# Two graph layers on one core: the first row of every adjacency loaded and split once, with a new order of all queues

## What is computed

```python
# x [128,128,512], adj [128,128,128]
# layer 0
h = maximum(layernorm(x), 0)
A_hat = adj + eye; d = A_hat.sum(-1) ** -0.5
x = x + (A_hat * d[:, :, None] * d[:, None, :]) @ (h @ W + b)

# layer 1
h = maximum(layernorm(x), 0)
H = (adj != 0); w = adj[:, 0, :]                 # row 0 of each adjacency: one weight per edge
Dn = where(H @ w > 0, 1 / (H @ w), 0); Be = 1 / H.sum(axis=1)
conv(x, W, b) = Dn * (H @ (Be * (H.T @ (x @ W.T)))) + b
h = relu(conv(h, W1, b1))                        # 512 -> 1024
h = layer_norm(h, gamma, beta)
out = conv(h, W2, b2) + x                        # 1024 -> 512
```

## Time and profile before

| | |
|---|---|
| median of 3 runs | 1931.68 us |
| the profiled execution | 1935.55 us |
| its span, first to last instruction | 1933.8 us |
| TensorE busy | 1874.0 us, 97% |
| DVE | 1634.2 us, 85% |
| ACT | 1445.4 us, 75% |
| POOL | 1189.7 us, 62% |
| DMA queues, share of 16 engines' span | 47.1% |
| mean granted clock of TensorE | 0.994 of full |

### The profile page before, as it was taken

The page is one execution under the profiler, slowest core; times in us unless marked ns, Lnnn a source line. Parts: engine busy times, 40 slices in busy tenths (PEclk is TensorE's granted clock), DMA queues, the critical chain, the costliest instruction groups (busy, mean ns, idle before and its releaser), DMA issues. The chain is left out here.

```text
span 1933.8 us, 37250 instructions
## 1 busy us (share of the span) xinstructions
PE 1874.0 (97%) x9926; PEld 895.9 (46%) x9926; DVE 1634.2 (85%) x3239; ACT 1445.4 (75%) x2726; POOL 1189.7 (62%) x1554
## 2 busy tenths in 40 slices
PE   5799999999999999999999999999999999999998
PEld 2344444444444444444444444444444444444443
DVE  6898888888888888888888888898888889788663
ACT  4787777777777778778778778778778778777663
POOL 4676666665665666666666666666666666566550
PEclk9899999999999999999999999999999999999999
DMA  7245554454454445544444454444454444454333
GB/s 220 46 84 109 110 107 99 102 107 99 103 112 97 102 111 101 101 109 102 102 106 101 102 109 99 102 113 96 101 111 99 101 106 109 89 108 98 70 66 77
DMA packets 536736, 197.59 MB, mean 102 GB/s; under 512 B 484944, under 2 KB 501328, under 8 KB 536528
## 3 DMA queue, kind: packets, MB, share of 16 engines
q1 hardware_dynamic: 536528, 195.21, 47.1%
HBM read 48.31 MB, written 33.55 MB: 42 GB/s over the span
## 5 line engine op out<-in xcount | busy, mean ns | idle before, releaser
L386 PE MATMUL ps_u<-w2h,raw_t 128*128 128x512 f16 x2048 | 483.9, 379 | 3.6 <-DVE raw_w L1060 3.0
L386 PEld LDWEIGHTS ps_u<-w2h,raw_t 128*128 128x128 f16 x2048 | 197.7, 98 | 232.3 <-issue 3.9
L715 ACT ACTIVATE raw_w<-raw_w 128x1024 f32<-128x1024 f32 x128 | 135.0, 1055 | 193.9 <-DVE raw_w L1011 193.1
L1423 POOL TENSOR_TENSOR base<-b_all,xh 128x512 f32<-128x512 f32 x128 | 187.1, 1462 | 90.9 <-DVE raw_w L1069 89.7
L386 PE MATMUL ps_u<-w2l,raw_t 128*128 128x512 f16 x1024 | 241.9, 379 | 0.0
L1417 POOL TENSOR_TENSOR b_all<-x,b_all 128x512 f32<-128x512 f32 x128 | 189.0, 1477 | 23.9 <-DVE x L974 13.8
L1438 POOL TENSOR_TENSOR tS<-tS 128x256 f32<-128x256 f32 x64 | 57.4, 897 | 214.4 <-ACT tS L695 214.4
L974 DVE SCALAR_TENSOR_TENSOR x<-ps_e,cx,x_t 128x512 f32<-128x512 f32 x128 | 95.0, 742 | 102.3 <-PE ps_e L439 102.2
L1055 DVE TENSOR_TENSOR bet_wide<-raw_w,bet_wide 128x1024 f16<-128x1024 f32 x128 | 157.4, 1230 | 15.1 <-ACT bet_wide L740 9.8
L1428 POOL TENSOR_TENSOR base<-base,raw_w 128x512 f32<-128x512 f32 x128 | 164.6, 1286 | 6.8 <-ACT raw_w L652 6.5
L731 ACT ACTIVATE raw_w<-raw_w,nm,sc 128x1024 f32<-128x1024 f32 x128 | 156.3, 1229 | 4.9 <-POOL nm L1499 4.9
(11 more groups left out here) (153 smaller groups left out, 4791.8 us busy)
## 6 DMA issues: line engine op xcount, KB each, us to landing
x_t<-in_x_dram SPq DMA_DIRECT2D x128, 256.0 KB, 3.0
out_dram<-raw_w SPq DMA_DIRECT2D x128, 256.0 KB, 2.3
adj_t<-in_adj_dram SPq DMA_DIRECT2D x64, 128.0 KB, 2.4
raw_t<-bet_wide SPq DMA_TRANSPOSE x256, 3.1
w_col<-in_adj_dram SPq DMA_DIRECT2D x128, 0.5 KB, 2.4
h0T_hi<-h_hi SPq DMA_TRANSPOSE x128, 2.4
h0T_lo<-h_lo SPq DMA_TRANSPOSE x128, 2.4
raw_w<-in_W1T_dram SPq DMA_DIRECT2D x4, 512.0 KB, 5.2
```

The source lines that it names most:

```text
L386: mm = pe.matmul(ps, t[:, j * 128:(j + 1) * 128], w[:, j, :], start=(n == 0 and j == 0), stop=(n == 2 and j == blocks - 1))
L715: act.activation(zh[:, g % 4, :], zh[:, g % 4, :], ACT.Relu, accum_out=hsum[:, p % 2, j:j + 1]).then_inc(s_h, 1)
L1423: pool.tensor_tensor(base[:, g % 6, :], x1b[:, :], xh[:, g % 2, :], ALU.add).then_inc(s_scr2, 1)
```

## The change

Row 0 of all 128 adjacencies is loaded in one transfer, graphs on the partitions, into the sixth slot of `base`. DVE splits it in two operations (hi and lo side by side in the same slot), and one transpose puts both halves of all graphs into a new tile WT, graph by graph in its columns. For each pair one copy, do_w(p), takes the four columns (hi and lo of two graphs) to column N of HB, a tile that now holds what HB_hi and HB_lo were. do_P(p) waits for that copy; the sixth slot of `base` is written for graph 5 by do_scr2 behind a wait for the transpose.

```diff
-    STEADY_FROM, STEADY_TO = 4, NP - 14
+    STEADY_FROM, STEADY_TO = 14, NP - 14
...
-        w_col = sb("w_col", [128, 3, 2])
+        WT = sb("WT", [128, 2, NG], F16)
...
-        HB_hi, HB_lo = sb("HB_hi", [128, 2, 2, N + 2], F16), sb("HB_lo", [128, 2, 2, N + 2], F16)
+        HB = sb("HB", [128, 2, 2, 2, N + 2], F16)
...
+        HB_hi, HB_lo = HB[:, 0, :, :, :], HB[:, 1, :, :, :]
+        w_rows = base[:, 5, 0:N]
+        w_halves = base[:, 5, N:2 * N].bitcast(F16).rearrange("p (h c) -> p h c", h=2)
...
+            def load_edge_weights():
+
+                sp.dma_start(w_rows, adj[:, 0, :]).then_inc(s_w, 16)
+
+            def turn_edge_weights():
+                sp.wait_ge(s_wrh, 1)
+                sp.wait_ge(s_wrl, 1)
+                sp.dma_start_transpose(WT[:, :, :], w_halves.rearrange("p h c -> p (h c)")).then_inc(s_wt, 16)
...
-            def do_ldw(p):
-                done(sp, s_wrl, p - 2)
-                for j in (0, 1):
-                    sp.dma_start(w_col[:, p % 3, j:j + 1], adj[2 * p + j:2 * p + j + 1, 0, :].rearrange("g e -> e g"))\
-                      .then_inc(s_w[p % 3], 16)
...
-            do_ldw(0); do_ldA(0); do_ldw(1); do_ldA(1); do_ldw(2); do_ldA(2); do_ldw(3); do_ldX(0); do_ldX(1)
-            do_ldA(3); do_trA(0)
+            do_ldA(0); do_ldA(1)
             load_weight(0, raw_w0, W, range(0, 4))
+            do_ldA(2); do_ldX(0); do_ldX(1)
             load_row(b_all, b, s_b)
             load_gamma_beta()
-            do_ldw(4); do_ldX(2); do_ldX(3); do_ldA(4); do_trA(1); do_tr0h(0); do_tr0h(1); do_tr0l(0); do_tr0l(1)
+            do_trA(0); do_ldA(3)
+            load_edge_weights()
+            do_trA(1); do_ldX(2); do_ldX(3); do_ldA(4)
             load_weight(1, raw_w1, W1T, range(0, 2))
             load_weight(1, raw_w1, W1T, range(2, 4))
-            do_ldw(5); do_ldA(5); do_trA(2)
+            do_ldA(5)
+            turn_edge_weights()
+            do_trA(2); do_tr0h(0); do_tr0h(1); do_tr0l(0); do_tr0l(1)
...
+            def split_edge_weights():
+                dve.wait_ge(s_w, 16)
+                dve.tensor_scalar(w_halves[:, 0, :], w_rows, WR_SCALE, None, ALU.mult).then_inc(s_wrh, 1)
+                dve.wait_ge(s_wrh, 1)
+                dve.scalar_tensor_tensor(out=w_halves[:, 1, :], in0=w_rows, scalar=WR_SCALE, in1=w_halves[:, 0, :],
+                                         op0=ALU.mult, op1=ALU.subtract).then_inc(s_wrl, 1)
...
-            def do_w_hi(p):
...
-            def do_w_lo(p):
...
+            def do_w(p):
+
+                if p == 0:
+                    dve.wait_ge(s_wt, 16)
+                done(dve, s_p, p - 1)
+                dve.tensor_copy(HB[:, :, p % 2, :, N], WT[:, :, 2 * p:2 * p + 2]).then_inc(s_wr, 1)
```

The tables of all five queues are new. The loop now covers k = 14 to 49, and ten of its former iterations are written out, with other orders. Its row on TensorE (M1, P, T1, ...) and its row on POOL read, in part:

```diff
-                do_M1(k); do_Y0(2 * k + 4); do_U(2 * k - 3); do_Y2(2 * k - 4); do_M5(k); do_M6(k); do_Y2(2 * k - 3)
...
+                do_M1(k); do_P(k+2); do_T1(2 * k + 2); do_Z0(2 * k + 7); do_M6(k); do_M5(k); do_M2(k)
+                do_Y0(2 * k + 8); do_Y2(2 * k - 3); do_M7(k); do_M3(k); do_T1(2 * k + 3); do_M4(k); do_Z0(2 * k + 8)
+                do_U(2 * k - 2); do_Y0(2 * k + 9); do_U(2 * k - 1); do_Y2(2 * k - 2)
```

More of the change, by code:

```diff
@@ L165, in bass_adjacency_prenorm_two_layer_gnn_kernel @@
         s_adj = [sem(f"adj_loaded_{m}") for m in range(3)]
-        s_w = [sem(f"edge_weights_loaded_{m}") for m in range(3)]
+        s_w, s_wt = sem("edge_weights_loaded"), sem("edge_weights_transposed")
         s_tra = [sem(f"A_and_H_transposed_{m}") for m in (0, 1)]
@@ L1190, in _ @@
+            split_lo_w1(range(0, 1))
+            do_bn0(4)
+            weight_magnitude(2)
+            do_aggr0(4); do_yv(1)
+            split_lo_w1(range(1, 2))
+            keep_beta_row()
+            do_yl(1)
             split_lo_w1(range(2, 3))
-            keep_beta_row()
-            weight_magnitude(2)
             split_lo_w1(range(3, 4))
+            do_x1(1)
+            split_lo_w1(range(4, 5))
+            do_st1(1)
+            split_lo_w1(range(5, 6))
+            do_Hu(5)
+            split_lo_w1(range(6, 7))
```

1008 lines of the change are left out of this document (572 added, 436 removed).

## The result

| | before | after |
|---|---|---|
| median | 1931.89 us (4 runs, 1931.12 to 1932.22) | 2025.81 us (4 runs, 2023.19 to 2027.48) |
| ratio, 95% interval | | 1.0483 (1.047 to 1.0495) |
| span of the profiled execution | 1933.8 us | 2025.1 us |
| mean granted clock | 0.994 | 0.994 |

What follows compares the result with a forecast made beforehand. TensorE, busy 97% of the span, was taken as the bound. Terms -7.3 - 1.0 + 1.0 - 1.5 = -8.8 us took the profiled 1935.55 to 1926.75; less 3.87 to the median, 1923 us, range 1916 to 1935.

Steps and rivals of the forecast that it cites:

- Term 1: Start up to M1(0): earlier W0 and W1 bring M1(0) to 70 us from 77.23; -7.3 us, bounds -3.8 and -8.6.
- rival 3: Start: P(0) waits for the transposed row, so the start gains less; 1925 to 1928 us, chance 0.04.
- rival 1: Start gives little: matmuls at 1.2 GHz, or a full DVE loses the gain by 70 us; 1928 us, chance 0.15.
- Term 2: From 77 to 213 us: new order fills TensorE's waits for tS and partly dn; -1.0 us, bounds -4 and +2.
- Term 3: Loop of 36 iterations: little room, so an overlap may cost in each; +1.0 us, bounds 0 and +10.8.
- The place with least room: Loop, behind U(2k-1): Y2(2k-3) can start 9.8 us after it, TensorE comes to it after 10.0; room 0.2 us.
- Rival 2: Loop: POOL's additions hold hn_lo or nearby DVE operations every iteration, 0.45 us excess times 36; 1938 us, chance 0.12.
- Term 4: Last 234 us: layer 0 through one pair earlier, P(63) between quarter products; -1.5 us, bounds -4 and +1.

Runs made afterwards that it cites:

- e1: The change's new way to load, split, transpose and copy row 0, with all queues in the orders of the kernel before; 1930.67 us, ratio 0.9992.
- e3: The changed kernel up to M1(0), from there the orders of the kernel before; 1931.61 us, ratio 1.0005.
- e10: The changed kernel up to its loop (k = 14), from there the orders of the kernel before; 1948.51 us, ratio 1.0093.
- e2: The changed kernel's queue orders, with the old small loads of w_col and their two DVE operations per pair back; 2048.72 us, ratio 1.0603.
- e11: The changed kernel with DVE's loop reordered: xh_lo and tlA behind nmu, x1, st1 and aggr1, ul directly behind them; 1999.44 us, ratio 1.0354.
- e13: As e11, but on DVE nmu(k) also stands behind x1, st1 and aggr1; 2060.08 us, ratio 1.0659.
- e17: The changed kernel with DVE's loop as in e13 and, on POOL, both biases directly behind rd0, then x1b(2k+4); 1975.72 us, ratio 1.0223.
- e5: The changed kernel's loop with uh(2k-2) ahead of h0_hi on ACT and ul(2k-2) ahead of HB_lo and h0_lo on DVE; 2024.36 us, ratio 1.0478.
- e8: The changed kernel's loop with out(2k-3) on DVE moved directly behind hn_lo(2k-1); 2023.67 us, ratio 1.0477.
- e14: As e13, with uh(2k-2) ahead of vq(2k+5) on ACT; 2036.7 us, ratio 1.0545.

## Why the prediction was wrong

**Term 1, the start: -7.3; -3.7 between the two profiles, and none is shown when all are taken together.** M1(0) stands at 73.49 in the kernel after and 77.23 before, but at 74.73 in e1 with the old orders and at 75.0 in the median of the new start, and the medians of e3 and before are level. The working rested on one profile, 3.7 us slower than its kernel's median. The sums hold up to the gram of W1: scale of W0 at 13.26 us (13 forecast), gram of W1 to 23.2 (22.8), Y0(0) at the low clock in 5.1 us (26.11 to 31.23); only the first matmul came sooner, at 4.86 (7 to 9). The sign of rival 3 was then seen, P(0) waiting 2.5 us for the copy out of WT, but not for its reason: the row landed at 22.13, near the 21.6 worked out, and the copy was held by POOL for 2.31 us. The scale of W1 came at 39.10 (36.2 forecast, 44.78 before), and the 2.9 us were never made up: M1(0) at 73.49 (70). That the lead at the scale of W1 is gone by M1(0) is what rival 1 said of a full DVE; no run tests that reason.

**Term 2, 77 to 213.4: -1.0, measured +3.0**, outside its bounds of -4 and +2: TensorE idles 11.8 us there (136.20 - 124.39) in place of 8.8. The two waits of the earlier trace rows went as worked out (that for tS is gone, P(3) keeps 0.7 of 1.2 us), but others are late next:

```profile
PE ps_e L411 <- DVE x L1063: 3.4, 2, 2.0
PE ps_z L422 <- issue: 2.3, 1, 2.3
PE ps_x L422 <- DVE raw_w L1100: 2.2, 4, 1.1
PE ps_y L462 <- DVE raw_w L1149: 1.9, 1, 1.9
```

x1, z and ul, all on a DVE that is as full as before (127.28 us). One more stop, of 2.3 us ahead of one quarter product (ps_z), has no releaser in the profile and stays unexplained. That what came late is the work of layer 0 that the new order brings forward fits pair 4, which is still 2.8 us ahead, but no run shows it.

**Term 3, the loop: +1.0, bounds 0 and +10.8. This is the step that failed**: measured +63.7 between pairs 14 and 49. Two things were wrong in it. First, the place: the working followed one consumer, Y2(2k-3), and rightly gave it little room; it lost 0.8 us in 36 iterations. That U(2k-1) needs ul(2k-2), and through it ACT's layer 0 and POOL's row of scalars, was not looked at, and neither was that the chain comes back to where it started. "The place with least room" can be found only when all links between two queues are followed around. Second, the size: the price per iteration was taken from the longest hn_lo of the kernel before (0.5 us, less 0.2 of room), and the hold was looked for on DVE alone. Rival 2, 1938 us, had the right kind of mechanism (DVE and POOL keep each other waiting, once per iteration) at 0.45 us, but only one way round, POOL's addition holding hn_lo, which is 0.3 us here; the larger part is DVE holding u1 and cx, 1.7 us. The measured loss is 1.82 us per iteration.

Its rule from the Trainium skill (SBUF — State Buffer, Who interferes with whom: a DVE instruction with two SBUF inputs and a GpSimd instruction that reads SBUF exclude each other for the whole instruction) agrees with the traces: u1 goes from 0.19 to 1.17, cx from 0.19 to 0.91, a bias from 0.26 to 2.13. The argument against rival 2, that POOL ran beside DVE in the old loop as well and TensorE lost nothing, was true and proved nothing: in the old loop one of the two biases took 1.52 us in every iteration, and TensorE idled 1.3 us in 35 iterations. A hold costs where the held instruction is on a chain as long as TensorE's work.

**Not in the sum at all: the written-out pairs 5 to 13.** They were taken to be no worse than the loop that they came from. TensorE idles 9.7 us more there than before (10.4 less 0.7), and e10 gives 17 us for all that precedes the loop. The 27.5 us that do_nmu falls back between pairs 4 and 14 overstate it: by the orders, an estimate, about 13 of them are the Y0 and Z0 of two more graph pairs done ahead (6.5 us each), not lost.

**Term 4, the end: -1.5.** Behind the loop TensorE idles 25.6 us where it idled 14.7 behind the same pair before. do_nmu falls back by another 19.4 us up to pair 59, at the pace of the loop, and gets 16.4 back by pair 63, where, it seems, the lead in layer 0 pays. The order of the tail by itself can't be priced from these runs.

**What stays open**: the 23 us by which e2 is above the kernel after, and the written-out pairs and the tail, which no run took apart. That the closed chain with its held instructions was the loop's cause rests on e11 (u1 and cx freed, 0.66 us less), e13 (longer holds on it lengthen the iteration) and e17 (biases early and xh_lo late, the late start of U, counted by the starts of the matmuls, falls from 1.6 to 0.27 us). e5 and e8 (moves of single links change nothing) agree with it only by the side links. No run took all holds away, so the 2.0 us that they cost by the table is an estimate. Where exactly it closes is shown only in the trace of the kernel after.

## What to carry to other kernels

Where each queue runs a fixed order and a loop repeats it, add up the chains that close over several engines within an iteration and set them against the bound engine's work in it: an engine that is only 59% busy, with instructions of two columns, can set the period. A move of one link against an equally long side link gains nothing, and a move that looks free can put another small instruction beside a long one; change the orders of both engines together. And the written-out part and the loop need a price each: what is "the same steps in another order" was 94 us here. A gain of a few us at the start can't be read from one profile of each kernel: M1(0) varied by 4.6 us between executions of the same start.

## What was not expected of the hardware

DVE and POOL hold each other up in both directions, for the whole of an instruction, and who is held goes by nanoseconds. In e14 POOL starts base2 (1.27 us) 10 ns ahead of hn_lo on DVE, and hn_lo takes 2.34 in place of 1.21; in e11 DVE is ahead by 20 ns, and POOL's takes 2.34. First e14, then e11, from the timelines:

```profile
1028.52 1.27 POOL L1569 TENSOR_TENSOR base<-base,raw_w 128x512 f32<-128x512 f32 x1
1028.53 2.34 DVE L1144 TENSOR_TENSOR bet_wide<-raw_w,bet_wide 128x1024 f16<-128x1024 f32 x1 [1.35 <-ACT bet_wide L781]
```

```profile
1043.77 1.23 DVE L1144 TENSOR_TENSOR bet_wide<-raw_w,bet_wide 128x1024 f16<-128x1024 f32 x1 [1.32 <-ACT bet_wide L781]
...
1043.79 2.34 POOL L1569 TENSOR_TENSOR base<-base,raw_w 128x512 f32<-128x512 f32 x1
```

A DVE instruction with one input was held as well: the fp16 copy of four columns out of WT took 2.31 us beside POOL's difference of W1 and 0.16 right behind it, and in the loop after one HB_hi of two takes 1.21 us in the median where it took 0.24 before. HB_hi alone adds 33 of the 56 us by which DVE is busier from pair 14 to 49. A held instruction usually gets its turn between two of the other engine's (u1 between xh_lo and tlA), so that instructions alternate; the bias in e13 did not and was held by both. Since a 10 ns shift decides who pays, an edit that makes one engine earlier can make the kernel slower, as e13 did by 61 us against e11.
